# A two-layer decoder on one core: the order of TensorE's side pieces in self-attention, and a transposing form for spread reciprocals in cross-attention

## The reference, cut to what matters

```python
attn = softmax(einsum('bhqd,bhkd->bhqk', q, k) * scale)
out = einsum('bhqk,bhkd->bhqd', attn, v)
```

## Time and profile before

| | |
|---|---|
| median of 3 runs | 769.81 us (769.68 to 770.94) |
| the profiled execution's own time | 769.94 us |
| its span, first to last instruction | 768.2 us |
| mean granted TensorE clock | 0.984 of full |
| PE busy | 710.7 us (93%) |
| ACT busy | 548.4 us (71%) |
| DVE busy | 491.7 us (64%) |
| POOL busy | 161.3 us (21%) |

### The profile page before, as it was taken

One profiled execution on the slowest core, in us unless ns is written; L12 is line 12 of the kernel. 1 busy time (PEld: TensorE's weight loads), 2 busy tenths in 40 slices (PEclk: granted clock), 3 DMA queues, 4 the chain that ended last, 5 costly groups with the idle time before them and its releaser, 6 DMA issues.

```text
span 768.2 us, 11057 instructions
## 1 busy us (share of the span) xinstructions
PE 710.7 (93%) x3946; PEld 397.3 (52%) x3946; DVE 491.7 (64%) x1165; ACT 548.4 (71%) x994; POOL 161.3 (21%) x224
## 2 busy tenths in 40 slices
PE   7989999999999999999999999889999899993897
PEld 5642222212222224889888887644656644441686
DVE  3885755753413224588437666758977787988786
ACT  2659999999999995464142435789887433799991
POOL 2652142201010000203253232333221100000022
PEclk9999999999999999999999999999999999997899
DMA  9113212131256151303236000001100000000002
GB/s 254 41 28 43 41 29 70 28 96 29 36 144 192 29 139 55 110 1 110 98 121 220 1 1 0 2 8 76 42 1 1 2 1 0 0 1 0 0 28 82
DMA packets 56973, 41.48 MB, mean 54 GB/s; under 512 B 37106, under 2 KB 53720, under 8 KB 56792
## 3 DMA queue, kind: packets, MB, share of 16 engines
q1 hardware_dynamic: 56744, 40.65, 19.3%
q10 hardware_dynamic: 176, 0.14, 0.1%
HBM read 27.94 MB, written 4.46 MB: 42 GB/s over the span
## 4 chain that ended last, share of the span: by engine, by line
PE 48%; ACT 26%; DVE 13%; issue 8%; POOL 2%; DMA 1%; SPq 0%; POOLq 0%; DVEq 0%; ACTq 0%
ACT arena L676 16%; PE banks L2230 8%; PE banks L1990 7%; PE banks L2006 6%; PE banks L1679 5%; PE banks L1665 2%; ACT arena L801 2%; DVE arena L1504 2%; DVE arena L1055 2%; PE banks L1851 2%; PE banks L2061 2%; PE banks L2118 2%; PE banks L1649 2%; PE banks L2090 1%; PE banks L2020 1%
## 5 line engine op out<-in xcount | busy, mean ns | idle before, releaser
L676 ACT ACTIVATE arena<-banks 128x1024 f32<-128x1024 f32 x256 | 236.6, 1164 | 4.1 <-PE banks L1665 4.0
L1679 PE MATMUL banks<-arena 128*32 128x512 f32 x1024 | 136.4, 604 | 3.0 <-DVE arena L1131 1.3
L1665 PE MATMUL banks<-arena 64*128 64x512 f16 x512 | 84.8, 383 | 5.4 <-ACT arena L676 1.6
L2230 PE MATMUL banks<-arena 128*128 128x512 f32 x192 | 83.1, 594 | 1.1 <-DVE arena L1520 0.9
L1665 PEld LDWEIGHTS banks<-arena 64*128 64x128 f16 x512 | 20.4, 93 | 102.1 <-ACT arena L676 92.5
L801 ACT ACTIVATE arena<-banks,arena 128x77 f32<-128x77 f32 x256 | 64.3, 365 | 11.4 <-DVE arena L1405 11.2
L429 POOL TENSOR_SCALAR arena<-arena 128x2 f32<-128x2 f32 (+2 forms) x39 | 11.8, 302 | 260.7 <-DVE arena L1058 260.7
L757 ACT ACTIVATE arena<-banks,arena 128x256 f32<-128x256 f32 x64 | 26.9, 471 | 49.3 <-PE banks L1990 49.3
L2230 PEld LDWEIGHTS banks<-arena 128*128 128x128 f32 x192 | 36.2, 190 | 47.4 <-issue 43.4
L2006 PE MATMUL banks<-arena 128*128 128x256 f32 x256 | 56.5, 380 | 1.2 <-ACT arena L698 1.2
L1990 PE MATMUL banks<-arena 128*128 128x256 f32 x256 | 56.2, 379 | 0.0
(11 more groups left out here) (264 smaller groups left out, 1237.7 us busy)
## 6 DMA issues: line engine op xcount, KB each, us to landing
arena<-in_L_ffn_w SPq DMA_DIRECT2D x16, 1024.0 KB, 7.5
w_kept<-arena SPq DMA_DIRECT2D x3, 768.0 KB, 3.6
arena<-w_kept SPq DMA_DIRECT2D x3, 768.0 KB, 4.9
arena<-in_x SPq DMA_DIRECT2D x4, 512.0 KB, 6.6
out_x<-arena SPq DMA_DIRECT2D x3, 512.0 KB, 2.9
arena<-in_L_ffn_b SPq DMA_DIRECT2D x1, 1024.0 KB, 12.5
arena<-in_L_ffn_w_gate SPq DMA_DIRECT2D x1, 768.0 KB, 6.7
arena<-in_L_ffn_w_up SPq DMA_DIRECT2D x1, 768.0 KB, 8.5
```

The source lines that it names most:

```text
L676: act.activation(PT[(TB * u + kt) % 3][:, half], PS[:, 2 * (n % 3):2 * (n % 3) + 2, :], ACT.Exp, scale=DH ** -0.5 / QK_UP ** 2).then_inc(s ...
L1665: mm = pe.matmul(bank(2 * (n % 3) + h), KT[u % 2][64 * h:64 * h + 64, P * kt:P * kt + P], QT[u % 2][64 * h:64 * h + 64, 512 * half:512 * h ...
L1679: mm = pe.matmul(PS[32 * j:32 * j + 32, 6, :], VS[w][:, kt, h, :], PT[(TB * u + kt) % 3][:, half, h, :], start=(kt == 0), stop=(kt == TB - 1))
L2230: mm = pe.matmul(bank(2 + n % 4), (wgT if n < IC * G4 else wuT)[:, k, P * c:P * c + P], XT[:, k, 512 * g:512 * g + 512], start=(k == 0), s ...
```

## The change

In cross-attention the sixth turn of `p_turn` becomes `pe.transpose(...)`, the form of the other five. In self-attention the first batch's output pieces move to steps 0, 3 (turns), 5 (divided rows) and 8, 9, 11, 13 (projection); a new function `between_keys` issues all side pieces, and `attn_unit` calls it ahead of the values in a unit's first key tile (`kt == 0`), behind them in the others and in the first key tile of unit 8. That moves the pieces at steps 0 and 8, `late_project`'s at step 8 among them. VectorE's `first_turned` moves from the odd unit to the end of the even one's pieces.

```diff
--- before.py
+++ after.py
@@ -60,6 +60,7 @@
 
 HT = 13
 SPREAD = {2: (0, 0), 4: (1, 0), 6: (0, 1), 8: (1, 1), 11: (0, 2), 13: (1, 2)}
+OUT_TURNS, OUT_ATT, OUT_PROJ = (0, 3), 5, (8, 9, 11, 13)
 
 UX = T * KD
 AHEAD = 3
@@ -1124,8 +1125,8 @@
                             out_norm(q - 1)
                         first_heads(q, 0)
                         first_heads(q, 1)
+                        first_turned(q)
                     else:
-                        first_turned(q)
                         out_residual(q, 7)
                 dve.wait_ge(sem("pv_done"), TB * u + TB)
                 dve.tensor_copy(OSB[:, u], bank(6)).then_inc(sem("o_evac"), 1)
@@ -1724,26 +1725,33 @@
                     mm.then_inc(sem("wo_mm"), 1)
 
             def first_out(q, step):
-                if step in (0, 5):
-                    first_turn(q, step // 5)
-                if step == 9:
+                if step in OUT_TURNS:
+                    first_turn(q, OUT_TURNS.index(step))
+                if step == OUT_ATT:
                     first_att_turn(q)
-                if 11 <= step < 15:
-                    first_proj(q, (step - 11) // 2, (step - 11) % 2)
+                if step in OUT_PROJ:
+                    first_proj(q, OUT_PROJ.index(step) // 2, OUT_PROJ.index(step) % 2)
+
+            def between_keys(u, step):
+                late = HT + u // 2
+                if late < T and step == 0:
+                    late_turn(late)
+                if late < T and step in SPREAD:
+                    late_project(late, *SPREAD[step])
+                if u >= NP:
+                    first_out((u - NP) // 2, step)
 
             def attn_unit(u):
                 for kt in range(TB):
                     for n in range(2 * (TB * u + kt) + 3, 2 * (TB * u + kt) + 5):
                         if n < 2 * TB * UN:
                             scores(n)
-                    late, step = HT + u // 2, TB * (u % 2) + kt
-                    if late < T and step == 0:
-                        late_turn(late)
+                    step = TB * (u % 2) + kt
+                    if kt == 0 and (u, step) != (NP, 0):
+                        between_keys(u, step)
                     values(u, kt)
-                    if late < T and step in SPREAD:
-                        late_project(late, *SPREAD[step])
-                    if u >= NP:
-                        first_out((u - NP) // 2, TB * (u % 2) + kt)
+                    if kt or (u, step) == (NP, 0):
+                        between_keys(u, step)
 
 
             def running(n):
@@ -2089,8 +2097,7 @@
                 for c, at in enumerate(P_AT):
                     pe.transpose(bank(4 + c // 4)[:, P * (c % 4):P * (c % 4) + P], e[:, at:at + P], ident)
                 pe.wait_ge(sem("xa_rd"), n + 1)
-                pe.matmul(bank(4 + NC5 // 4)[:, P * (NC5 % 4):P * (NC5 % 4) + P], rdS[n % 4], ident,
-                          start=True, stop=True).then_inc(sem("xa_ptr"), 1)
+                pe.transpose(bank(4 + NC5 // 4)[:, P * (NC5 % 4):P * (NC5 % 4) + P], rdS[n % 4], ident).then_inc(sem("xa_ptr"), 1)
 
             def xa_values(g, k, half=None):
                 b0, cols = VALUES_IN[half]
```

## The result

| | before | after |
|---|---|---|
| median | 769.97 us (769.68 to 770.94, 4 runs) | 762.33 us (761.41 to 763.01, 4 runs) |
| profiled execution's span | 768.2 us | 760.6 us |

The ratio is 0.9900, with a 95% interval of 0.9888 to 0.9912: 7.7 us less, between 6.8 and 8.6. Forecast were 761.7 us, with 757.8 to 766.3.

The account below looks back on a forecast made before the run. ScalarE's exponentials set self-attention's pace, TensorE's lateness costing 8.3 us; in cross-attention the chain passes between engines. 5.6 + 1.1 + 1.5 = 8.2 us off 769.94 gave 761.7 us, range 757.8 to 766.3.

Parts of the forecast that it names:

- Edits 1 and 2: Self-attention: pieces ahead of values in units' first key tiles, and output pieces spread wider, together gain 5.6 of 8.3 us.
- the neighbouring pair: Self-attention projection pieces in consecutive tiles, steps 8 and 9: a loss of 0.2 us a pair, bounds 0 and 0.41.
- the tile takes 0.54 + 0.63 + 1.00 = 2.17: A self-attention unit's first key tile: scores, covered piece and values take 2.17 us, not 2.64 to 2.68.
- still 0.35 lost at steps 9, 11 and 13: Sign of being wrong, in self-attention: each of these projection steps still loses 0.35 us.
- That the parts are additive: Self-attention: gains of 1.3, 1.65 and 2.65 us from reordering and spreading pieces were summed to 5.6 us.
- Edit 2's waits: Self-attention: the wider spread tightens TensorE's waits for VectorE, but none should last; margins 1.8 us and more.
- rival E: Self-attention: a turn waiting behind VectorE blocks TensorE, 0.35 us a pair, 1.4 in all, 763.1 us; chance 0.05.
- The tail: End of self-attention: with the last projection piece at step 13, 0.4 + 0.7 = 1.1 us are gained.
- The transposing form: Cross-attention: one instruction for two saves 0.11 us in each of 32; 16 on the chain, 1.5 us taken.
- Rival A: Self-attention: ScalarE's idle time is all there is to gain; 6.2 us less in all, 763.7 us; chance 0.12.
- B: Cross-attention: the transpose's gain is hidden because the released engine meets another wait; 763.2 us; chance 0.10.
- C: Cross-attention: further falls of TensorE's clock give back 1.7 us each, from five on slower, 770.2 us; chance in full 0.03.
- D: Cross-attention: with other idle times one or both clock falls go, 760.0 or 758.3 us; chance 0.10.

Follow-up runs that it names:

- form only: The kernel before with only cross-attention's sixth turn made a transpose, self-attention unchanged: 769.24 us, ratio 0.9983.
- apart, warmer, filled: Changed kernel with projections at 7, 9, 11, 13, very first turn ahead of its values, 17 warming matmuls, eight unread matmuls before item 30's scores: 757.85 us, ratio 0.9855.
- order only: The changed kernel without the transposing form, so both self-attention edits with the fp32 product kept: 763.29 us, ratio 0.9913 against the kernel before.
- border only: The kernel before with side pieces ahead of values in a unit's first key tile, old output steps and fp32 product kept: 767.59 us, ratio 0.9969.
- spread: The kernel before with the output's pieces at the new steps, all behind their values, fp32 product kept: 765.93 us, ratio 0.9960.
- two products: The kernel before with one of cross-attention's five transposes made an fp32 product too: 770.23 us, ratio 1.0000.

## Why the prediction came out right

The forecast was 0.6 us off, and that it came so near is partly luck. The edits' own parts, 4.63 + 1.05 + 1.6 = 7.3 us by the profiles, fall 0.9 short of the 8.2 forecast. The start, one fall less and the longer last stage, none of them in the sum, add -1.5 - 1.7 + 2.9 = -0.3 in the profile.

**Edits 1 and 2** were put at 5.6 us and gave 4.63. The term that was mis-sized is the neighbouring pair, steps 8 and 9: 0.2 taken, 0.41 given as the bound, 0.06 + 0.34 = 0.40 measured (the exponential behind step 9's piece comes 0.34 us late in each of the four pairs). ScalarE of the kernel after at two neighbouring exponentials, 1.25 us apart instead of 0.905:

```profile
192.01 1.23 ACT L677 ACTIVATE arena<-banks 128x1024 f32<-128x1024 f32 x1
193.26 1.02 ACT L677 ACTIVATE arena<-banks 128x1024 f32<-128x1024 f32 x1
```

Times four that is 0.8 of the missing 1.0. In the last pair the spread saved about 0.2 where 0.4 was taken, and the very first turn costs about 0.6 where it cost 0.54. The reason given for the low value was the order of before, a border and then a turn at step 9, which loses nothing. The sentence that failed is "the tile takes 0.54 + 0.63 + 1.00 = 2.17": it takes 2.46, since TensorE, when ahead, spends part of the covered half microsecond waiting for ScalarE's banks. The border pieces of the late projections, where TensorE comes late, did fall from 0.50 to 0.07 each, a little better than the 0.1 left. Of the signs of being wrong, "still 0.35 lost at steps 9, 11 and 13" came true for step 9 alone; 11 and 13 lose 0.06 each.

**That the parts are additive** was assumed and is wrong in detail: alone they give 2.55 and 2.64, which is 5.2, and together 4.63.

**Edit 2's waits** held: among TensorE's waits in self-attention none is for `first_heads` or `first_turned`, and rival E is out.

**The tail**, 1.1 forecast, is 1.05.

**The transposing form**, 1.5 forecast, is 1.6 at equal clock. The path to it was partly lucky: the chain held the product 16 times before and only 10 times after, so "16 x 0.11" is no count of the ones that matter. The Trainium skill (TensorE: Matmul & The Clock Gate, Terms) has the transposing mode four times faster for fp32; the trace has 0.11 us against 0.22, a factor of two.

**Rival A** (idle time is all) is out: 4.63 us gained where 4.1 stood idle, with 0.6 idle left. **B** is out by "form only".

**C and D, the clock.** A fall in cross-attention costs 1.5 to 1.7 us, about as forecast (the one at 504 in "apart, warmer, filled" only 0.6), and that the change makes them more or fewer isn't seen: with the product the six profiles (before twice, order, border, spread, two products) have 2, 1, 1, 0, 1 and 0 falls in cross-attention, with the transposing form the seven have 0 ("form only") and 1 in each of the others. The Trainium skill, TensorE: Matmul & The Clock Gate, Part 4: PE-mode transpose, says that transposes don't count as activity in the way products do; five falls in six profiles against six in seven, with one turn of six changed, neither show it nor rule it out. At one place the change may matter: ahead of item 30's scores TensorE idles for 1.7 us with the product (1.3 with two products) and for 2.17 with the transposing form. The clock fell behind that idle time in two of six profiles with the product (before at 583.0, "order only" at 574.5) and in five of the six unfilled ones with the form. That leans to C, and is too few to show it. What the prediction left out was the last stage. The changed kernel's 157.5 us in both profiles, against 154.6 and 156.0, took back 1.5 to 2.9 us, and in the profile the shorter start and one fall less made up for it: -1.5 - 4.6 - 1.0 - 3.35 + 2.9 = -7.6.

Left open: why a stretch that idles alike ends in a fall in one profile and not in another (as in "form only"), how often the last stage's second fall comes without a profile, and why the medians of "form only", "border only" and "two products" lie 3 to 6 us above their profiled executions.

## What to carry to other kernels

Where one engine's instructions overlap, measure its pace by the distance of starts in an undisturbed stretch, and price each lateness against it; idle and busy shares show half of it at most. A wait covers a piece only as far as nothing else has grown into it: look at the tile in the state in which the engine will come to it, early or late, not in the one it has now. And compare a stage at equal granted clock before giving a microsecond to an edit.

## What the runs showed of the hardware

Two things I had not expected. An exponential of 128x1024 is recorded with 1.02 us when it starts on an idle engine and with up to 1.68 us far into an undisturbed stretch, at the same distance of 0.904 us between starts: the record lengthens from one exponential to the next while none is held up. It doesn't tell how early the scores were there. The one of 1.68 us, at 175.06 us of the kernel after, had them 0.6 us before its start, and one of 1.23 us, at 188.35, had them 1.1 us before. And a clock that rises early can be lost again: where it rose early in the warming of ten, the ten matmuls were done early, the idle time behind them grew from 3.6 to 4.7 us, and the clock that they had raised fell again, at a cost of 1.3 to 2.9 us.
